# The last pair of heads of an attention layer: four half phases made into two whole ones

## The chip, the cores and the metric

One core of a Trainium2 chip runs the whole program. The metric is the device time of one execution in microseconds (us). In the text PE is the matmul engine (TensorE), DVE is VectorE, ACT is ScalarE, POOL is GpSimd, and SP is the queue that issues most DMAs. An engine works through its own instruction stream in program order and waits on semaphores for the others.

## What is computed

Two layers on x of shape (2, 1024, 128), each an attention-like part and a feed-forward part, all in fp32. The change lies in the first part of the first layer, full attention with 16 heads of 64 channels over each of the two sequences:

```python
Q = jnp.einsum('btd,hkd->bthk', x, W_Q) + b_Q      # K and V alike, x layer-normed
scores = jnp.einsum('bqhk,bshk->bhqs', Q, K) / jnp.sqrt(d_head)
attn = jax.nn.softmax(scores, axis=-1)
out_h = jnp.einsum('bhqs,bshk->bqhk', attn, V)
x = x + jnp.einsum('bqhk,hdk->bqd', out_h, W_O) + b_O
```

Behind it follow a routed feed-forward part with 8 experts (each row of x goes to one), a state-space part and a dense feed-forward part with 8 experts.

## The kernel before

**Pairs and phases.** Heads are taken two at a time: 8 pairs for each sequence, pairs 0 to 15. Pair 15 is `LAST`. The 1024 queries of a pair are two chunks `c` of 512, and the 1024 keys are eight blocks `j` of 128. A step `("score", pair, c, j)` makes the scores of a key block against a query chunk for both heads of the pair (`pe_score`, eight matmuls, lines 583 and 587). ACT exponentiates them in one instruction of 128x1024 (`act_score`, line 1072) into one of ten buffers `prob`. A step `("pv", pair, c, j)` multiplies them by the values and adds to the output bank `A.O` (`pe_pv`, line 615). After the eighth, `take` copies that bank to `oraw` on ACT (line 1081). One pair and chunk with its eight scores and eight value products is a phase (`phase`).

**Normalising.** The sum over the keys of the exponentials is made elementwise first: seven additions of 128x1024 for a phase, one for each `j` from 1 to 7. POOL makes them for pairs 0 to 14 (`pool_score`, line 2014) and DVE for pair 15 (`dve_late_sums`, line 1690, run at the place of the step `pv` in DVE's order). `("sumhalf", pair, c)` is a set of 32 very small matmuls over that sum (`pe_sum_half`, line 665), which needs all seven additions, and a reciprocal on DVE (line 1542). `("out", pair, c)` is the output projection (`pe_out`, line 679, 16 small matmuls) and eight DVE instructions that scale it by the reciprocal and add it to x (`dve_out`, line 1556).

**Order.** One list, `K.order`, written out by hand, says in which order every engine takes its steps: each engine walks the same list and runs what is its own. So moving a step in the list moves it in the stream of PE, of DVE, of ACT, of POOL and of SP. For pairs 0 to 14 a phase has eight scores and then eight value products, with other steps between the value products. These include the projections and maxima for later pairs. The last pair has none of those left. Its list is written by `last_phase(f)` for f = 0 to 3: four scores, four value products, each time. The two output projections of pair 14 both stand behind the scores of f = 1.

**Side steps of the routed part.** Between the value products stand steps from `EARLY` for the routed feed-forward of the first sequence: `turn` is a transpose of gathered rows on PE (line 732), `turned` its copy by ACT (line 1156), and `fetch` is a DMA of an expert's weights, 578 KB, issued by SP (line 2194). Fetches 6 to 12 also wait for a score of pair 15 each (`FETCH_BEHIND`).

**Banks.** PSUM is used as four double banks, slots 0 to 3. Scores and output projections of pair 15 turn through slots 0, 1 and 2 (`slot_of`), and each waits until ACT or DVE has emptied what was in its slot before. The single bank 7 serves `turn`, `sumhalf` and the like one after another.

**After the last pair.** `routed_order` goes on with this list:

```python
order = [("after", "scores"), ("up", 0), ("gelu", 0), ("sumhalf", LAST, 1), ("lnhalf", 3), ("out", LAST, 1), ("up", 1), ("gelu", 1),
         ("fetch", 13), ("after", "attention"), ("pad",), ("lnvar", 3), ("lnroot", 3), ("down", 0), ("yrow", 0), ("fetch", 14)]
```

`up` and `down` are an expert's two products (lines 745 and 756), `yrow` adds a bias on DVE (line 1662). `lnhalf` and `lnvar` are DVE's statistics of x for the layer norm of the second sequence (lines 1464, 1452 and 1456). `lnroot` on POOL and `lnrows` on DVE (line 1473) finish it, and `lnturn` on PE (line 569) transposes the normed rows.

Of the kernel before, what the change touches and what calls it, by code (L numbers as in the profile page):

```python
# [16 lines left out]
NT = SEQ // P  # L17
AT = B * NT
CH = 512
NC = SEQ // CH  # L20
# [48 lines left out]
LAST = PAIRS - 1  # L69
# [109 lines left out]
def turned(n):  # L179

    return [("lnturn", n, 0), ("lnturn", n, 1), ("lncopy", n, 0), ("lncopy", n, 1)]
# [6 lines left out]
def largest(*maxes):  # L188

    return [step for m in maxes for step in (("max", *m), ("maxed", *m))]  # L190


def phase(pair, c):


    last, nxt, ahead = pair - 1, pair + 1, pair + 2
    maxes = [(nxt, *m) for m in MAXES[NT * c:NT * (c + 1)]]
    chunks = [chunk for chunk in CHUNKS[2 * c:2 * c + 2] if ahead < PAIRS and (ahead, *chunk) not in STAGED]
    first, second = ([*map(lambda chunk: project(ahead, chunk), chunks)] + [[], []])[:2]
    pv = [("pv", pair, c, j) for j in range(NT)]  # L200
    early = [EARLY.get((pair, 2 * c + i), []) for i in range(2)]
    order = []
    for j in range(NT):
        order += largest(maxes[j]) + [("score", pair, c, j)]
    if c == NC - 1:
        order.append(("cols", nxt))
    if last >= 0:
        order.append(("out", last, c))
    order += first[:1] + pv[:1] + first[1:] + pv[1:3] + second[:1] + pv[3:4] + second[1:] + pv[4:5]
    if c == NC - 1:  # L210
        order += [("row", nxt), ("rowed", nxt)] + pv[5:6] + [("values", nxt, 1), ("valued", nxt, 1)] + early[0] + pv[6:7] + [("sumhalf", pair, 0)]
    else:
        order += [("values", nxt, 0), ("valued", nxt, 0)] + pv[5:6] + early[0] + pv[6:7] + [("sumhalf", last, NC - 1)] * (last >= 0)
    return order + pv[7:] + [("take", pair, c)] + early[1]


def slot_of(step):

    kind, pair, *k = step
    if kind == "max" and pair:  # L220
        return 0 if k[0] % 2 == 0 else 3
    if kind == "score" and pair < LAST:
        return 1 + k[1] % 2
    if kind == "out" and pair < LAST - 1:
        return 0
    if kind == "score":
        return (2 + k[1]) % 3 if k[0] == 0 else k[1] % 3
    if kind == "out":
        return (2, 0)[k[0]] if pair == LAST else 1 + k[0]


def last_phase(f):

    pair, c, js = LAST, f // 2, range(NT // 2 * (f % 2), NT // 2 * (f % 2 + 1))
    order = [("score", pair, c, j) for j in js]
    if f == 1:
        order += [("out", pair - 1, 0), ("out", pair - 1, 1)]
    second = ([("sumhalf", pair, 0)] if f == 3 else []) + EARLY.get((pair, f), [])
    pv = [("pv", pair, c, j) for j in js]
    order += pv[:2] + second + pv[2:3] + [("sumhalf", pair - 1, NC - 1)] * (f == 0) + pv[3:]  # L240
    if f % 2:
        order.append(("take", pair, c))
    if f == 3:
        order.append(("out", pair, 0))
    return order


def ahead_of_scores(pair, chunk):
    return [("proj", pair, *chunk), ("full", pair, *chunk)]


def attention_order():

    order = [("gsum",), ("lnvar", 0), ("lnroot", 0), ("gscale",), ("lnrows", 0), *turned(0), ("bias", 0)]
    keys, queries, more_keys, more_queries = (("proj", 0, *ch) for ch in CHUNKS)
    maxes = [(0, *m) for m in MAXES]
    order += [keys, queries, *largest(*maxes[:2]), more_keys, more_queries, *largest(*maxes[2:4])]
    order += [("full", 0, *ch) for ch in CHUNKS] + largest(maxes[4]) + ahead_of_scores(1, CHUNKS[0]) + largest(*maxes[5:7])
    order += ahead_of_scores(1, CHUNKS[1]) + largest(*maxes[7:9]) + [("values", 0, 0)] + largest(*maxes[9:11])
    order += ahead_of_scores(1, CHUNKS[2]) + largest(*maxes[11:13]) + ahead_of_scores(1, CHUNKS[3]) + largest(maxes[13])  # L260
    order += [("values", 0, 1)] + largest(maxes[14]) + ahead_of_scores(2, CHUNKS[0]) + largest(maxes[15])
    order += [("gdir",), ("cols", 0), ("row", 0), ("valued", 0, 0), ("rowed", 0), ("valued", 0, 1)]
    for pair in range(LAST):
        for c in range(NC):
            order += phase(pair, c)
    for f in range(4):
        order += last_phase(f)
    return order


# [116 lines left out]
def whole_order():  # L387
    return attention_order() + routed_order() + first_inputs_order() + recurrence_order() + dense_order()
# [48 lines left out]
def plan_all(K):  # L437
# [7 lines left out]
    for step in K.order:  # L445
# [15 lines left out]
        elif step == ("after", "state"):  # L461
            work.take_turns(0, 6)
            for bank in range(2, 8):
                work.held.pop(bank, None)
        elif kind == "score":
            plan_slot(K, "act", step, slot_of(step))
            if k[2]:
                (K.psum_late if k[0] == LAST else K.psum_done).plan(*k)
        elif kind == "max":
            plan_slot(K, "dve", step, slot_of(step) if k[0] else 1 + len(K.slots.place) % 2, now=False)  # L470
        elif kind == "maxed":
            K.slots.plan_empty("max", *k)
        elif kind == "out":
            plan_slot(K, "dve", step, slot_of(step))
        elif kind in ("sumhalf", "gdir"):
            work.plan("dve", *step)
# [2046 lines left out]
```

## Time and profile before

| | before |
|---|---|
| median of three runs | 1172.74 us |
| the three runs | 1172.57, 1172.74, 1174.8 us |
| the profiled execution: its own time | 1174.9 us |
| its span in the profile | 1173.6 us |
| mean granted TensorE clock in it | 0.983 |
| PE busy | 1099.0 us, 94% of the span |
| DVE busy | 828.6 us, 71% |
| ACT busy | 619.2 us, 53% |
| POOL busy | 761.6 us, 65% |

The profile is of one execution, the table's third row, and its times count from the span's start. The last pair of heads takes the stretch from 707.26 to some 749 us. Start and duration of matmuls come from the profile, their ends are modelled, so the distance from one start to the next is the better measure.

### The profile page before, as it was taken

What the parts mean: (1) busy time and instruction counts of PE and PEld (TensorE: products, weight loads), DVE (VectorE), ACT (ScalarE), POOL (GpSimd) and SP (SyncE); (2) the same over time, 40 slices, a digit from 0 to 9 for tenths busy, and PEclk for the clock granted to TensorE, in tenths of its full rate; (3) what the DMA queues carried; (4) which work ended last, traced back from release to release, by engine and by line L of the source; (5) the groups of instructions that cost most, each with busy time, mean ns of one, the idle gap of its engine ahead of it and who ended that gap; (6) DMA issues with size and microseconds to landing.
All of it is one profiled execution on the core that took longest, in us unless ns stands there. A gap on an engine that the chain in (4) does not pass through costs nothing.

```text
span 1173.6 us, 19598 instructions
## 1 busy us (share of the span) xinstructions
PE 1099.0 (94%) x7549; PEld 676.2 (58%) x7549; DVE 828.6 (71%) x1223; ACT 619.2 (53%) x867; POOL 761.6 (65%) x393
## 2 busy tenths in 40 slices
PE   5899998999999998999999999978879988899998
PEld 1456565556556565556665655877535434445786
DVE  4757665667657666656676755624798999998887
ACT  3545354535435445535443534545985664856753
POOL 3588877687877877686778980041289897996200
PEclk9999998999999999999999999989899999999999
DMA  6000000000000000000000115356564444341000
GB/s 202 2 1 2 1 1 1 2 1 1 2 1 1 2 1 1 2 1 2 1 1 7 44 40 198 106 169 206 161 213 144 161 148 141 130 164 47 11 9 18
DMA packets 38076, 68.85 MB, mean 59 GB/s; under 512 B 5952, under 2 KB 24128, under 8 KB 37984
## 3 DMA queue, kind: packets, MB, share of 16 engines
q1 hardware_dynamic: 34976, 64.52, 17.2%
q0 software_dynamic: 1024, 2.10, 0.5%
q8 instruction: 60, 0.98, 0.3%
q10 hardware_dynamic: 1984, 0.98, 0.3%
q14 instruction: 32, 0.26, 0.1%
HBM read 61.30 MB, written 6.16 MB: 57 GB/s over the span
## 4 chain that ended last, share of the span: by engine, by line
PE 73%; POOL 8%; issue 7%; DVE 7%; ACT 3%; DMA 2%; POOLq 0%; SPq 0%; ACTq 0%; DVEq 0%
PE psum L615 18%; PE psum L583 14%; PE psum L599 5%; PE psum L631 5%; PE psum L587 5%; PE psum L981 3%; PE psum L887 3%; POOL psums L2014 3%; PE psum L964 3%; PE psum L665 2%; POOL hc L2102 2%; PE psum L679 2%; PE psum L646 2%; DVE mx L1501 2%; PE psum L756 2%
## 5 line engine op out<-in xcount | busy, mean ns | idle before, releaser
L2014 POOL TENSOR_TENSOR psums<-psums,prob 128x1024 f32<-128x1024 f32 x180 | 427.8, 2377 | 26.7 <-POOL psums L2014 1.3
L1501 DVE TENSOR_REDUCE mx<-psum 128x2 f32<-128x1024 f32 x256 | 300.9, 1225 | 55.6 <-PE psum L599 55.1
L1072 ACT ACTIVATE prob<-psum 128x1024 f32<-128x1024 f32 x256 | 261.5, 1027 | 70.2 <-PE psum L587 47.2
L615 PE MATMUL psum<-prob,V 128*64 128x512 f32 x1024 | 246.4, 597 | 0.0
L2102 POOL TENSOR_TENSOR hc<-hs,cc 128x1024 f32<-128x1024 f32 x64 | 151.7, 2371 | 21.2 <-DVE hs L1789 18.6
L2014 POOL TENSOR_TENSOR psums<-prob 128x1024 f32<-128x1024 f32 x30 | 72.1, 2404 | 122.7 <-ACT prob L1072 122.7
L1789 DVE TENSOR_TENSOR_SCAN hs<-dA,psum 128x1024 f32<-128x1024 f32 x64 | 146.4, 2287 | 2.2
L615 PEld LDWEIGHTS psum<-prob,V 128*64 128x64 f32 x1024 | 67.7, 137 | 102.1 <-issue 98.2
L887 PE MATMUL psum<-hc,ident 128*128 128x512 f32 x256 | 123.3, 605 | 2.5 <-DVE slot_rows_h L1797 1.4
L583 PE MATMUL psum<-q_hi,k_hi 64*128 64x512 f32 x512 | 108.6, 411 | 8.4 <-ACT prob L1072 8.4
L599 PE MATMUL psum<-k_hi,q_hi 64*128 64x512 f32 x512 | 110.0, 418 | 4.5 <-DVE mx L1501 1.6
L587 PE MATMUL psum<-guard,row_one 64*128 64x512 f32 x512 | 104.7, 395 | 0.7 <-DMA guard<-mrow 0.7
L1081 ACT COPY oraw<-psum 128x512 f32<-128x512 f32 x32 | 18.8, 588 | 163.1 <-PE psum L615 163.1
L583 PE MATMUL psum<-q_hi,k_lo 64*128 64x512 f32 x512 | 104.8, 396 | 0.0
L583 PE MATMUL psum<-q_lo,k_hi 64*128 64x512 f32 x512 | 104.8, 396 | 0.0
L1556 DVE SCALAR_TENSOR_TENSOR x<-psum,inv,x 128x128 f32<-128x128 f32 x256 | 72.0, 345 | 21.4 <-PE psum L679 15.5
L599 PEld LDWEIGHTS psum<-k_hi,q_hi 64*128 64x128 f32 x512 | 51.6, 189 | 42.6 <-issue 27.1
L887 PEld LDWEIGHTS psum<-hc,ident 128*128 128x128 f32 x256 | 48.5, 193 | 44.6 <-issue 32.4
L583 PEld LDWEIGHTS psum<-q_hi,k_hi 64*128 64x128 f32 x512 | 49.9, 188 | 41.8 <-ACT prob L1072 26.1
L871 PE MATMUL psum<-xdr,pickr 128*128 128x512 f32 x128 | 57.7, 533 | 10.8 <-DVE hs L1789 10.6
L1494 DVE SCALAR_TENSOR_TENSOR q_lo<-psum,bq,q_hi 128x512 fp32r<-128x512 f32 x28 | 21.0, 751 | 60.8 <-ACT q_hi L1046 60.8
L1046 ACT ACTIVATE q_hi<-psum,bq 128x512 fp32r<-128x512 f32 x32 | 22.0, 689 | 78.6 <-PE psum L631 78.6
(287 smaller groups left out, 1746.6 us busy)
## 6 DMA issues: line engine op xcount, KB each, us to landing
cc<-C_rows SPq DMA_DIRECT2D x64, 512.0 KB, 3.7
kq_wts<-in_e_rows SPq DMA_DIRECT2D x14, 578.0 KB, 4.9
e_wts<-in_e_rows SPq DMA_DIRECT2D x10, 578.0 KB, 4.5
e_w<-in_e_rows SPq DMA_DIRECT2D x6, 578.0 KB, 4.8
slots_in<-e_zero SPq DMA_DIRECT2D x2, 960.0 KB, 8.4
slots_out<-e_y SPq DMA_DIRECT2D x30, 64.0 KB, 3.2
x<-in_x SPq DMA_DIRECT2D x2, 512.0 KB, 4.9
e_w<-in_e_w SPq DMA_DIRECT2D x1, 1024.0 KB, 7.7
```

Of the source, the lines that this page charges most:

```text
L583: pe.matmul(both[:, s, :], left[HALF[s], js], right[HALF[s], cs], start=(part == 0), stop=False)
L587: ins = pe.matmul(both[:, s, :], A.row_one[HALF[s], :], A.guard[q][HALF[s], cs], start=False, stop=True)
L599: ins = pe.matmul(both[:, s, :], A.q_hi[r][HALF[s], t * P:(t + 1) * P], A.k_hi[r][HALF[s], c * CH:(c + 1) * CH], start=True, stop=True)
L615: ins = pe.matmul(A.O[HALF[s], :], A.V[pair % 2][:, j, s * DH:(s + 1) * DH], A.prob[unit(pair, c, j) % NPB][:, s * CH:(s + 1) * CH], start ...
L631: ins = pe.matmul(bank[HALF[s], :], w[:, (2 * p + s) * DH:(2 * p + s + 1) * DH], K.xnT[:, b, c * CH:(c + 1) * CH], start=True, stop=True)
L887: ins = pe.matmul(X.Y[:, c * CH:(c + 1) * CH], K.ident[:, :], X.hc[u % 3][:, c * CH:(c + 1) * CH], start=(u > 0 and n == 0), stop=(n == NS ...
L1072: act.activation(A.prob[n % NPB][:, :], slots.bank("score", pair, c, j).rearrange("p s n -> p (s n)"), ACT.Exp, scale=float(DH) ** -0.5).t ...
L1501: dve.tensor_reduce(K.A.mx[:, :, t, c], slots.bank("max", pair, t, c), AXX, ALU.max).then_inc(*slots.inc("max", pair, t, c))
L1556: ins = dve.scalar_tensor_tensor(out=K.x[:, tile, :], in0=slots.bank("out", pair, c)[:, s, t * P:(t + 1) * P], scalar=A.inv[:, s * NT + 4 ...
L1789: dve.tensor_tensor_scan(X.hs[u % 3][:, :], X.dA[u % 3][:, :], X.gain[u % 2], 0.0, ALU.mult, ALU.add).then_inc(X.state_done, 1)
L2014: pool.tensor_tensor(total[:, :], (K.A.prob[(n - 1) % NPB] if j == 1 else total)[:, :], K.A.prob[n % NPB][:, :], ALU.add).then_inc(*K.psum ...
L2102: pool.tensor_tensor(X.hc[u % 3][:, :], X.hs[u % 3][:, :], X.cc[u % NCC][:, :], ALU.mult).then_inc(X.product_done, 1)
```

## The change

The last pair gets two phases. Each has all eight scores, then one output projection of pair 14, then eight value products. The side steps are the same ones, put between these value products. The reciprocal sums of pair 14 and 15 and the copies stay at the same value products or move by one. The slots change with it: scores of chunk 0 take slot j % 3 where they took (2 + j) % 3, and both output projections of pair 14 take slot 2 where they took 1 and 2.

```diff
     if kind == "score":
-        return (2 + k[1]) % 3 if k[0] == 0 else k[1] % 3
+        return k[1] % 3
     if kind == "out":
-        return (2, 0)[k[0]] if pair == LAST else 1 + k[0]
-
-
-def last_phase(f):
-
-    pair, c, js = LAST, f // 2, range(NT // 2 * (f % 2), NT // 2 * (f % 2 + 1))
-    order = [("score", pair, c, j) for j in js]
-    if f == 1:
-        order += [("out", pair - 1, 0), ("out", pair - 1, 1)]
-    second = ([("sumhalf", pair, 0)] if f == 3 else []) + EARLY.get((pair, f), [])
-    pv = [("pv", pair, c, j) for j in js]
-    order += pv[:2] + second + pv[2:3] + [("sumhalf", pair - 1, NC - 1)] * (f == 0) + pv[3:]
-    if f % 2:
-        order.append(("take", pair, c))
-    if f == 3:
-        order.append(("out", pair, 0))
-    return order
+        return (2, 0)[k[0]] if pair == LAST else 2
+
+
+def last_phase(c):
+
+    pair = LAST
+    order = [("score", pair, c, j) for j in range(NT)]
+    pv = [("pv", pair, c, j) for j in range(NT)]
+    early = [EARLY[pair, 2 * c + i] for i in range(2)]
+    if c == 0:
+        return order + [("out", pair - 1, 0)] + pv[:2] + early[0] + pv[2:3] + [("sumhalf", pair - 1, NC - 1)] + pv[3:5] + early[1] + pv[5:] + [("take", pair, c)]
+    order += [("out", pair - 1, 1)] + pv[:2] + [("sumhalf", pair, 0)] + early[0] + pv[2:6] + early[1] + pv[6:]
+    return order + [("take", pair, c), ("out", pair, 0)]
...
-    for f in range(4):
-        order += last_phase(f)
+    for c in range(NC):
+        order += last_phase(c)
```

## Rows read from the trace of the kernel before

**Rows 1.** The page: its first line.

```profile
span 1173.6 us, 19598 instructions
```

**Rows 2.** Busy time by stretch: us, PE, PEld, DVE, ACT, POOL, clock, DMA share, GB/s.

```profile
707.26:726.30 19.04, 19.04 (x170) 11.35 (x168) 8.26 (x21) 9.22 (x11) 0.00 (x0) 1.00 0.67 228
726.30:742.11 15.81, 15.81 (x131) 8.90 (x129) 12.30 (x12) 8.14 (x9) 0.00 (x0) 1.00 0.37 113
```

**Rows 3.** The chain of waits behind the last pair: start, duration, what.

```profile
746.18 0.39 DVE stats L1464 x2
...
746.58 1.14 DVE x L1556 x4
...
754.84 0.66 PE psum L569 x4
...
781.34 3.84 DMA slots_out<-e_y
```

**Rows 4.** PE in order of time, pair 15: start, duration, line, tiles.

```profile
716.41 0.51 PE L583 MATMUL psum<-q_hi,k_hi 64*128 64x512 f32 x2
...
717.46 0.40 PE L583 MATMUL psum<-q_hi,k_hi 64*128 64x512 f32 x2
...
720.21 1.95 PE L679 MATMUL psum<-wo,oraw 64*128 64x128 f32 x32
722.09 1.94 PE L615 MATMUL psum<-prob,V 128*64 128x512 f32 x8
723.95 0.55 PE L732 MATMUL psum<-ident,slot_rows_h 128*128 128x128 f32 x3
...
726.30 0.50 PE L583 MATMUL psum<-q_hi,k_hi 64*128 64x512 f32 x2
...
730.15 3.65 PE L615 MATMUL psum<-prob,V 128*64 128x512 f32 x16
733.74 0.50 PE L583 MATMUL psum<-q_hi,k_hi 64*128 64x512 f32 x2
...
742.11 1.16 PE L679 MATMUL psum<-wo,oraw 64*128 64x128 f32 x16
...
744.28 1.10 PE L665 MATMUL psum<-ones,psums 128*64 128x1 f32 x32
745.31 1.16 PE L679 MATMUL psum<-wo,oraw 64*128 64x128 f32 x16
```

**Rows 5.** PE in order of time, a single output projection in phase 14.

```profile
695.37 1.07 PE L679 MATMUL psum<-wo,oraw 64*128 64x128 f32 x16
696.36 4.51 PE L615 MATMUL psum<-prob,V 128*64 128x512 f32 x20
```

**Rows 6.** DVE in order of time.

```profile
721.72 4.48 DVE L1556 SCALAR_TENSOR_TENSOR x<-psum,inv,x 128x128 f32<-128x128 f32 x16 [4.80 <-issue]
726.12 5.20 DVE L1690 TENSOR_TENSOR psums<-psums,prob 128x1024 f32<-128x1024 f32 x4
731.24 1.22 DVE L1690 TENSOR_TENSOR psums<-prob 128x1024 f32<-128x1024 f32 x1
...
740.45 0.21 DVE L1542 RECIPROCAL inv<-psum 128x8 f32<-128x8 f32 x1 [1.86 <-PE psum L665]
740.58 2.51 DVE L1690 TENSOR_TENSOR psums<-psums,prob 128x1024 f32<-128x1024 f32 x2
743.37 2.29 DVE L1556 SCALAR_TENSOR_TENSOR x<-psum,inv,x 128x128 f32<-128x128 f32 x8 [0.28 <-PE psum L679]
```

**Rows 7.** ACT in order of time, the exponentials of four scores.

```profile
727.53 3.78 ACT L1072 ACTIVATE prob<-psum 128x1024 f32<-128x1024 f32 x4 [0.53 <-PE psum L587]
```

**Rows 8.** PE in order of time, just ahead of a stretch at half clock.

```profile
574.61 2.08 PE L708 MATMUL psum<-e_wgu,xnT 128*128 128x8 f32 x16
```

**Rows 9.** Busy time by stretch, as rows 2, at full and at half clock.

```profile
576.60:580.00 3.40, 3.40 (x19) 2.68 (x20) 2.86 (x8) 0.84 (x1) 0.00 (x0) 0.54 0.00 0
703.00:706.00 3.00, 2.12 (x34) 1.35 (x32) 0.69 (x1) 0.59 (x1) 2.86 (x2) 1.00 0.26 58
```

## The prediction

> **What bounds the kernel now.** I read the page first, then the busy time of the last pair's stretch, then the chain of waits behind it, and last the streams of PE, DVE and ACT one by one. The span is 1173.6 us [rows 1], and the profiled execution took 1174.9 us by its own time, 1.3 more than its span. That is 2.2 above the median of the three runs, at the top of their range. I work out a difference against this execution and put it on the median.
>
> In pair 15 PE never rests: it is busy in all 19.04 us of the first stretch and in all 15.81 us of the second, at the full clock [rows 2]. So up to the last value product every 0.1 us of PE counts. DVE has 8.26 busy us in the first stretch and 12.30 of 15.81 in the second. The reader is to see that DVE is no bound as a share, but has little left in the second. From 746.18 the chain has left PE: it runs over DVE's statistics, DVE's last output projection (746.58) and the layer norm until PE's transposes at 754.84 [rows 3]. What makes DVE late in that stretch makes the kernel late. The chain goes on through the routing of the second sequence to the store of the last expert row at 781.34, and those steps hang on each other, so I see no slack there.
>
> **What goes from PE.** No matmul is removed. What goes is changing between kinds of matmul. A score costs 0.917 us in a run ((720.21 - 717.46) / 3), but the first costs 1.05 [rows 4]. Four scores and the change to value products take 730.15 - 726.30 = 3.85. Four value products take 3.59 before scores follow. Two in the middle cost 3.59 - 1.86 = 1.73, with 1.86 from 722.09 to 723.95, so 0.865 each. Two half phases are 2 x (3.85 + 3.59) = 14.88. One whole is 3.85 + 4 x 0.917 + 3.59 + 4 x 0.865 = 14.57. That is 0.31 saved for each chunk, 0.62 in all. The two projections of pair 14 took 1.88 together (720.21 to 722.09). A single one takes 0.99 [rows 5], so two cost 1.98, and I count 0.05 of that 0.10 as a change that the scores no longer pay (3.80 into a projection, 3.85 into a value product). PE gains 0.57, call it 0.6. Bounds: 0.3 if only one side of each change is saved, 0.9 if the parts around the transposes gain too.
>
> PE would then start the second phase's scores at 726.30 - 0.31 (one phase merged) - 0.89 (one projection moved behind, 1.88 - 0.99) = 725.1, and its projection of pair 15 at 742.11 - 0.57 = 741.5.
>
> The Trainium skill, "TensorEngine Tiling (Array Packing)", section Key Properties, says that changing the tiling mode drains TensorE. By that rule alone, which speaks for the change, the kernel would be faster by the drains; the trace agrees in sign, and the sum by its own rows is the 0.6 above. This is the rival "gain" below.
>
> **What moves on DVE.** This decides. In the new list the projection of (14, 1) stands behind eight scores and ahead of all value products of chunk 1. DVE runs the seven additions of the chunk at the places of the value products. So all seven are queued behind DVE's part of that projection, though the first exponentials are there 6 us earlier. Before, both projections stood in the first chunk, and DVE started chunk 1's additions at 731.24 [rows 6].
>
> Step by step: eight scores from 725.1 take 3.80 + 4 x 0.917 = 7.47, so PE's projection starts at 732.57. DVE starts 1.26 after such a start (742.11 to 743.37, with an idle 0.28 ended by PE) [rows 4, 6], at 733.8. Eight of its instructions take (726.12 - 721.72) / 2 = 2.20, to 736.0. An addition has a pitch of (731.24 - 726.12) / 4 = 1.28, seven take 8.96, and the reciprocal among them takes 0.13 (740.45 to 740.58). Then DVE comes to the projection of (15, 0) at 745.1. Before it was 743.37. That is 1.7 later. With the first chunk DVE is done in time: its projection starts at about 716.0, seven additions and a reciprocal end at 727.3, and it then idles for 6.5 us.
>
> Who waits: PE comes to the last `sumhalf` at 741.5 + (744.28 - 742.11) = 743.7 and needs the last addition at 745.1, so PE idles 1.4. It starts its last projection some 1.03 later (744.28 to 745.31), at 746.1, and DVE could take that at 747.4. DVE itself is ready only 746.58 - 743.37 = 3.21 after 745.1, at 748.3. So the 1.4 on PE is not added to the 1.7; the chain of rows 3 starts 1.7 late, and with it `lnrows`, the transposes at 754.84 and all that follows. The part of PE's 0.6 that is gained ahead of DVE's last projection start is already in the 1.7, through the 725.1. Sum: +1.7. Bounds: +1.3 (DVE starts 0.1 sooner after PE, PE gains 0.9) and +2.1 (PE gains 0.3, DVE 0.1 slower).
>
> **Edits that cost nothing.** ACT takes 3.78 / 4 = 0.945 for an exponential [rows 7], a little more than a score on PE. Over eight scores it falls 0.2 behind. A score needs only the exponential three before it: the eighth starts 6.5 after the first, and that exponential ends 1.23 + 5 x 0.945 = 5.96 after it (1.23 from 726.30 to 727.53). The margin is 0.5; if it goes, PE waits by what is missing. Slot 2 for the projection needs the sixth exponential, 6.9 after the first score, and PE comes at 7.47. The second transpose and the reciprocal share bank 7: PE needs it at about 721.7 and DVE's reciprocal is done at about 721. If that were late, PE would lose the lateness. The slots of chunk 0 were empty long before. The weight fetches on SP keep their order and only come sooner, since the scores that they wait for do. DMA share is 0.67 and 0.37 in the two stretches [rows 2], and the first use of the earliest of them is in the sixth expert slot behind the pair.
>
> **The rivals.** (1) Likeliest, 0.60: DVE is late, +1.7, so 1174.4 us, 0.14% over the median, inside what is told from no change (0.2%, 2.3 us).
>
> (2) Gain, 0.15: the additions are no bound, because DVE starts them sooner than I reckon or because what follows absorbs 1.7. For it speaks DVE's idle time; against it that DVE's stream is in order and that rows 3 show no idle step up to 781.34. It would show -0.6, 1172.1 us. It decides if DVE's additions end before 743.7.
>
> (3) The other side, 0.20: slower by more than 0.2%, through the clock. PE's idle 1.4 at 743.7 is followed by `sumhalf`, 32 matmuls of one column. In the trace PE did 2.0 us of 128x8 matmuls at 574.61 [rows 8], and then came 3.4 us at a granted clock of 0.54 [rows 9], near the lower of the two levels (1.2 GHz, not 2.4). Against it: an idle 0.9 in the stretch 703 to 706 (PE busy 2.12 of 3.00) left the clock at 1.00. If 3.4 us at half clock fall behind 754.84, where PE is in the chain, they cost half of that, 1.7, and the sum is +3.4: 1176.1 us. If they fall at once behind the wait, DVE's chain hides most (PE has 748.3 - 747.4 = 0.9 to spare there), and the sum stays near +2.1. It decides when the added cost passes 0.6.
>
> The Trainium skill, "TensorE: Matmul & The Clock Gate", section "Part 1: The HAM clock gate", says that the clock is halved after idling and regained by sustained work. The trace agrees at rows 9, and nothing before the change shows what it makes of a wait like this one.
>
> (4) The remaining 0.05: something else, such as the exponentials or bank 7 holding PE by several tenths in each phase, or a transfer that comes in another order downstream.
>
> **How the numbers follow.** The time is that of the first case, 1172.74 + 1.7 = 1174.4. The runs shown lie 2.2 apart, so a median may sit 1 to 2 us off. The range goes from just under the gain to just over the third case: 1171.9 to 1176.8. Slower by over 0.2%: 0.17 from case 3, 0.12 from the upper end of case 1, 0.01 else: 0.30. Faster: 0.03 from case 1 and 0.05 from case 2: 0.08. Within: 0.62.
>
> **What would show it.** Right if in the profile after, PE's second phase starts at about 725.1, DVE idles about 6.5 us ahead of the second projection, its last addition ends near 745.1, the last `sumhalf` on PE has an idle time of about 1.4 ended by line 1690, and the transposes of line 569 that ended the chain start near 756.5. Wrong if the additions start ahead of DVE's projection, if PE idles within the eight scores (line 1072 as the releaser), or if the granted clock falls between 743 and 760. The time would be wrong, with the steps right, if the distance from 754.84 to the end changes by more than 1 us.

## The result and the profile after

The changed kernel takes 1175.17 us (median of 12 runs, 1173.87 to 1177.46); the kernel before, beside it on the same chip, 1172.65 us (12 runs, 1168.91 to 1174.8). The ratio is 1.0026, 95% interval 1.0013 to 1.0038. It is 0.26% slower, some 3 us (the two medians lie 2.5 apart), a little past the 0.2% that I had set as the bound of no change. The interval reaches from 0.13 to 0.38%, so on which side of that bound it lies is not settled. The forecast was 1174.4 with 62% on no change and 30% on slower.

The page after, its first line:

```profile
span 1173.7 us, 19598 instructions
```

That is within 0.1 us of the span of before [rows 1], and would mislead. In this execution the pair's first score starts at 704.83, before it started at 707.26, although the same work stands ahead of it. So I measure from that first score. I call S its start and T the start of the second transpose of the layer norm, where the chain leaves DVE for PE. Before, T - S is 754.84 - 707.26 = 47.58 us. After, it is 754.37 - 704.83 = 49.54. From S to the end it was 466.34 and is 468.87, 2.53 more: 1.96 up to T, 0.57 behind it.

Line numbers of the kernel after are four smaller than those of before in this part, so its 1686 is 1690 before. PE after, in order of time (start, duration, line, tiles, and in brackets the idle time and what ended it):

```profile
704.83 0.50 PE L579 MATMUL psum<-q_hi,k_hi 64*128 64x512 f32 x2
...
705.87 0.41 PE L579 MATMUL psum<-q_hi,k_hi 64*128 64x512 f32 x2
...
711.33 0.41 PE L579 MATMUL psum<-q_hi,k_hi 64*128 64x512 f32 x2
...
712.24 1.07 PE L675 MATMUL psum<-wo,oraw 64*128 64x128 f32 x16
...
722.56 0.49 PE L579 MATMUL psum<-q_hi,k_hi 64*128 64x512 f32 x2
...
729.96 1.05 PE L675 MATMUL psum<-wo,oraw 64*128 64x128 f32 x16
730.94 1.94 PE L611 MATMUL psum<-prob,V 128*64 128x512 f32 x8
732.71 1.05 PE L661 MATMUL psum<-ones,psums 128*64 128x1 f32 x32
733.61 5.35 PE L611 MATMUL psum<-prob,V 128*64 128x512 f32 x24
738.89 1.16 PE L675 MATMUL psum<-wo,oraw 64*128 64x128 f32 x16
739.98 1.16 PE L741 MATMUL psum<-slotT,e_wts 128*128 128x128 f32 x8
742.57 1.10 PE L661 MATMUL psum<-ones,psums 128*64 128x1 f32 x32 [1.43 <-DVE psums L1686]
743.60 1.16 PE L675 MATMUL psum<-wo,oraw 64*128 64x128 f32 x16
744.69 2.08 PE L741 MATMUL psum<-slotT,e_wts 128*128 128x128 f32 x8
746.56 1.80 PE L752 MATMUL psum<-e_wts,slot_rows_h 128*128 128x128 f32 x8
748.20 1.06 PE L741 MATMUL psum<-slotT,e_wts 128*128 128x128 f32 x8
```

Eight scores and a projection go through without an idle step. The projection of (15, 0) starts 738.89 - 704.83 = 34.06 after S, where it was 34.85 [rows 4]. Then PE idles 1.43 for the last addition, and two steps behind that its matmuls take double. The `up` at 744.69 lasts 1.87 to the next start, and the one at 748.20 lasts 0.89.

DVE after:

```profile
713.42 2.29 DVE L1552 SCALAR_TENSOR_TENSOR x<-psum,inv,x 128x128 f32<-128x128 f32 x8 [9.18 <-PE psum L675]
...
718.27 6.54 DVE L1686 TENSOR_TENSOR psums<-psums,prob 128x1024 f32<-128x1024 f32 x5
731.12 2.29 DVE L1552 SCALAR_TENSOR_TENSOR x<-psum,inv,x 128x128 f32<-128x128 f32 x8 [6.31 <-PE psum L675]
733.32 1.22 DVE L1686 TENSOR_TENSOR psums<-prob 128x1024 f32<-128x1024 f32 x1
...
734.64 7.87 DVE L1686 TENSOR_TENSOR psums<-psums,prob 128x1024 f32<-128x1024 f32 x6
742.43 2.28 DVE L1552 SCALAR_TENSOR_TENSOR x<-psum,inv,x 128x128 f32<-128x128 f32 x8
```

The reader is to see the 6.31 of idle time ended by PE's projection, with all seven additions behind it. DVE comes to the projection of (15, 0) at 37.60 after S, where it was 36.11 [rows 6].

The busy time by stretch, first up to the last value product's end and then to T (us, PE, PEld, DVE, ACT, POOL, clock, DMA share, GB/s), and a narrower stretch behind the wait:

```profile
722.56:738.89 16.33, 16.33 (x146) 10.10 (x144) 9.57 (x16) 8.03 (x9) 0.00 (x0) 1.00 0.38 110
738.89:754.37 15.48, 13.84 (x143) 13.16 (x141) 13.02 (x48) 7.75 (x23) 2.05 (x4) 0.89 0.31 89
...
744.80:748.20 3.40, 3.40 (x17) 3.40 (x17) 3.26 (x15) 1.14 (x4) 0.14 (x2) 0.51 0.48 135
```

Granted clock 0.51: that is the lower level, 1.2 GHz. The chain of waits shows what it did:

```profile
743.67 1.09 PE psum L675 x16
744.76 2.00 PE psum L741 x8
746.77 1.59 PE psum L752 x8
...
751.04 0.91 PE psum L752 x8
...
751.97 0.29 DVE e_y L1658
752.26 2.06 DVE xrows L1469 x8
```

Before, the chain in this place ran over DVE and POOL alone, from 746.18 to 754.80. Rows 3 leave out these two pieces of it:

```profile
750.94 1.68 POOL rstd L1964
752.64 2.15 DVE xrows L1473 x8
```

Now it runs over PE at half clock: DVE's bias step for an expert row (line 1658) stands ahead of `lnrows` in DVE's stream and waited for PE's `down`.

### The profile page after: what moved, and what is told of

Read it like the earlier page. It is cut to its first block, busy times and chain, and to the rows that moved or that the text cites. A ratio compares the mean times of both kernels' runs of the same rounds, so it can differ in the third digit from the quotient of the medians.

```text
span 1173.7 us, 19598 instructions
## 1 busy us (share of the span) xinstructions
PE 1098.3 (94%) x7549; PEld 677.3 (58%) x7549; DVE 827.8 (71%) x1223; ACT 618.0 (53%) x867; POOL 760.8 (65%) x393
## 4 chain that ended last, share of the span: by engine, by line
PE 72%; POOL 8%; DVE 8%; issue 7%; ACT 3%; DMA 2%; POOLq 0%; SPq 0%; DVEq 0%; ACTq 0%
PE psum L611 17%; PE psum L579 14%; PE psum L595 5%; PE psum L627 5%; PE psum L583 5%; PE psum L977 3%; PE psum L883 3%; POOL psums L2010 3%; PE psum L960 3%; POOL hc L2098 3%; PE psum L661 2%; PE psum L642 2%; PE psum L675 2%; DVE mx L1497 2%; PE psum L752 2%
```

## The experiments

The experiments ran on three chips: e1 to e4 on one, where the kernel before took 1178.68 us (median of 35 runs), e5 to e8 on a second (1179.81, 35 runs), and e9 to e12, one run each, on a third, where the one run of the kernel before took 1180.76. In the groups of 35 the kernel before ran from 1175.3 to 1181.5. Ratios are against it on the same chip. Since that scatter is as large as the effects, T - S in each profile is the finer measure. Up to T it repeats to within 0.05 us wherever the clock stays full. The kernel before has a profile on the first chip only. e4 has its order on PE, and there PE comes to the projection of (15, 0) 34.80 us after S, where before has 34.85.

| run | ratio, 95% interval | PE's wait | clock behind it | T - S |
|---|---|---|---|---|
| before | | none | full | 47.58 |
| changed, first | 1.0026 [1.0013, 1.0038] | 1.43 | half, 3.4 us | 49.54 |
| e1 changed again | 1.0016 [1.0001, 1.0031] | 1.43 | full | 48.94 |
| e8 changed, third | 0.9999 [0.9985, 1.0014] | 1.42 | half, 6.8 us | 51.07 |
| e9 changed, fourth | one run | 1.42 | half, 3.4 us | 49.49 |
| e2 DVE's additions first | 0.9983 [0.9969, 0.9996] | none | full | 46.79 |
| e7 the same again | 0.9987 [0.9971, 1.0002] | none | full | 46.74 |
| e3 up fills the wait | 1.0003 [0.9990, 1.0016] | 0.53 | full | 48.94 |
| e10, e11 the same | one run each | 0.54, 0.53 | full | 48.95, 48.90 |
| e4 before, DVE late by two additions | 1.0015 [1.0000, 1.0031] | none at sumhalf | full | 49.69 |
| e5 half phases, projection moved | 1.0006 [0.9995, 1.0017] | none | full | 48.12 |
| e6 whole phases, projection in chunk 0 | 0.9993 [0.9982, 1.0004] | none | full | 47.05 |
| e12 changed, longer wait | one run | 2.69 | half, 6.8 us | 52.07 |

**e1, e8, e9: the changed kernel again.** No edit.

> The changed kernel again, for a second profile beside the others. Theory 1 (DVE's additions stand behind its projection, and PE's wait for them lowers the clock): from the start of the pair's first score DVE comes to the projection of (15, 0) at 37.6 us, PE waits 1.4 us ahead of the last sumhalf, and a stretch of half clock begins within 3 us of that wait, as in the first profile. Total 2 to 3 us over the kernel before. Theory 2 (the stretch of half clock there was chance): the same 37.6 and 1.4, the clock stays full behind the wait, and the total is still 2 to 3 us over.

> The changed kernel a third time. The transposes at 48.9 to 49.0 us after the first score if the clock stays full behind PE's wait, and at 49.5 if it falls there, which happened once in two profiles. Total 1.4 to 3 us over before.

> The changed kernel, a fourth profile, for the clock behind PE's wait alone. In three profiles the wait was 1.43 us each time, and in two of them a stretch of half clock began within 3 us behind it, of 3.4 and 6.8 us. Theory 1 (the wait brings it, by where it falls): again a wait of 1.43, and a stretch of half clock in about two of three. Rival (chance, anywhere): none.

DVE's lateness and PE's wait came the same each time: 37.60, 37.59, 37.59, 37.59 us after S, and 1.42 or 1.43. The clock did not. In e1 it stayed full, as theory 2 of the first expectation had it; in e8 and e9 it fell, as in theory 1. In e1 T - S was 48.94, which is 1.36 over before. In e8 it fell for 6.8 us, from 0.8 us behind the end of the wait:

```profile
743.98 1.24 PE L661 MATMUL psum<-ones,psums 128*64 128x1 f32 x32 [1.42 <-DVE psums L1686]
745.15 2.08 PE L675 MATMUL psum<-wo,oraw 64*128 64x128 f32 x16
747.15 2.07 PE L741 MATMUL psum<-slotT,e_wts 128*128 128x128 f32 x8
749.02 1.91 PE L752 MATMUL psum<-e_wts,slot_rows_h 128*128 128x128 f32 x8
...
757.32 0.66 PE L565 MATMUL psum<-ident,xrows 128*128 128x128 f32 x4 [0.21 <-DVE xrows L1469]
```

T - S of e8, 51.07, lies outside both values that I had expected for it. So what the change costs up to T is 1.36 for DVE and 0, 0.6 or 2.1 for the clock. The timing of e8 (0.9999, its upper end 1.0014) came out lower than I expected, and its median of 1180.04 lower than its own profiled run (1182.45). Its interval still meets those of the other two timings, that of the first only by a hair, and the three together (mean of all runs less the mean of the kernel before: 3.0, 1.6 and 0.4 us) agree with 1.4 to 3 only loosely.

**e2, e7: DVE alone in another order.** PE, ACT and SP are those of the changed kernel. DVE alone takes two steps behind the last addition: its part of the projection of (14, 1) and the reciprocal of (15, 0). No run moves one without the other.

```diff
+def dve_order(order):
+
+    late = [("out", LAST - 1, 1), ("sumhalf", LAST, 0)]
+    order = [step for step in order if step not in late]
+    at = order.index(("pv", LAST, NC - 1, NT - 1)) + 1
+    return order[:at] + late + order[at:]
...
-    for kind, *k in K.order:
+    for kind, *k in dve_order(K.order):
```

> PE, ACT and SP keep the new order. DVE alone takes the seven additions of the last chunk before its part of the projection of (14, 1) and the reciprocal of (15, 0). Theory 1: DVE's additions end about 30.5 us after the pair's first score, PE waits nowhere and keeps full clock, the projection of (15, 0) is bound by PE at 34.1 + 1.2 = 35.3, and the kernel is 0.6 to 0.8 us faster than before, some 3 faster than the changed one. Rival (the loss comes from the runs of eight scores or from the clock by chance, not from DVE's order): the time stays within 1 us of the changed kernel, 2 to 3 over before.

> The kernel of the second experiment again: its first timing gave 0.17% under before, 2.0 us, and its trace only 0.8 us at the layer norm's transposes. Theory 1: the transpose again at 46.8, and the time 0.5 to 1 us under before, so that two timings together lie nearer 0.8 than 2. Rival (a gain elsewhere too): again 2 us.

DVE in e2:

```profile
727.76 1.23 DVE L1686 TENSOR_TENSOR psums<-prob 128x1024 f32<-128x1024 f32 x1 [0.96 <-ACT prob L1068]
729.09 7.87 DVE L1686 TENSOR_TENSOR psums<-psums,prob 128x1024 f32<-128x1024 f32 x6
736.88 2.28 DVE L1552 SCALAR_TENSOR_TENSOR x<-psum,inv,x 128x128 f32<-128x128 f32 x8
...
742.15 2.29 DVE L1552 SCALAR_TENSOR_TENSOR x<-psum,inv,x 128x128 f32<-128x128 f32 x8 [2.87 <-issue]
```

The additions now wait for an exponential and not for the projection. They end 30.1 after S in place of 37.7. DVE then idles 2.87 ahead of the projection of (15, 0). The profile names no releaser there, but the start lies 1.27 behind PE's, as it does where PE is named (1.26 in rows 4 and 6). PE has no idle step up to the transposes, and T - S is 46.79: 0.79 less than before and 2.15 less than in e1. The two timings give 0.9983 and 0.9987, 2.0 and 1.5 us under before; only the first excludes 1, and its interval includes 0.8 us. So my expectation for e7 missed: the two together lie nearer 2 than 0.8. Whether something behind T gains too is open. Up to T the order of DVE's steps alone turns a gain of 0.79 into a loss of 1.36. The rival that the runs of eight scores cost something falls.

**e3, e10, e11: PE's wait filled, DVE as late as ever.**

```diff
-    order = [("after", "scores"), ("up", 0), ("gelu", 0), ("sumhalf", LAST, 1), ("lnhalf", 3), ("out", LAST, 1), ("up", 1), ("gelu", 1),
+    order = [("after", "scores"), ("up", 0), ("gelu", 0), ("up", 1), ("gelu", 1), ("sumhalf", LAST, 1), ("lnhalf", 3), ("out", LAST, 1),
```

> The changed kernel with the second expert's up and gelu ahead of the last sumhalf, so that PE has 1.1 us of matmuls in the 1.4 us of its wait. DVE's lateness is untouched. Theory 1: PE's idle time falls to about 0.3, the clock stays full, the transposes of the layer norm come 0.5 us sooner (49.0 in place of 49.5 us after the pair's first score), the kernel is 0.5 to 1 us faster than the changed one and still 1.5 slower than before. Rival (DVE's lateness costs nothing, the PE wait is the whole loss): at most 0.5 slower than before.

> The kernel with the second up ahead of the last sumhalf, second profile. DVE's lateness is the same, PE's wait 0.5. Theory 1: full clock from the last pair to the transposes at 48.9. Rival: half clock as often as in the changed kernel.

> The same kernel, third profile: by theory 1 full clock and 48.9 once more.

PE in e3:

```profile
740.95 2.05 PE L741 MATMUL psum<-slotT,e_wts 128*128 128x128 f32 x16
743.53 1.10 PE L661 MATMUL psum<-ones,psums 128*64 128x1 f32 x32 [0.53 <-DVE psums L1686]
...
750.75 1.13 PE L752 MATMUL psum<-e_wts,slot_rows_h 128*128 128x128 f32 x8 [1.11 <-DVE e_y L1658]
```

T - S is 48.94, the same as in e1, though 0.9 of the wait is gone. The time that PE won came back as a wait for DVE at the third `down`, 1.11 where e1 has 0.36 there. So up to T PE's wait costs nothing in itself; DVE's lateness is what is paid. The timing does not decide this: it is 0.03% over before, 0.4 us, where I expected 1.5 and the rival at most 0.5, and its interval (-1.2 to +1.9 us) holds both. The idle time fell to 0.53 and not to the 0.3 that I expected, and my expectation of a T at 49.0 compared with the profile at half clock. The clock stayed full in all three.

**e4: DVE late and nothing else.** The kernel before, with two idle additions behind the last:

```diff
+    if (c, j) == (NC - 1, NT - 1):
+        dve.wait_ge(*K.psum_late.at(pair, c, j))
+        for _ in range(2):
+            dve.tensor_tensor(A.psums[0][:, :], total[:, :], A.prob[n % NPB][:, :], ALU.add).then_inc(*K.dve_own.inc())
+            dve.wait_ge(*K.dve_own.now())
```

> The kernel before, with two more additions of 128x1024 on DVE behind the last one, ahead of its projection of (15, 0); their result is read by nobody. PE's sumhalf does not wait for them. Theory 1 (the chain behind the pair runs over DVE): 2 x 1.3 - 0.3 of slack = 2.3 us slower. Rival (what follows absorbs DVE's lateness; only PE's wait costs): within 0.5 of before.

```profile
744.14 2.48 DVE L1695 TENSOR_TENSOR psums<-psums,prob 128x1024 f32<-128x1024 f32 x2
746.66 2.29 DVE L1556 SCALAR_TENSOR_TENSOR x<-psum,inv,x 128x128 f32<-128x128 f32 x8
```

DVE's projection starts 38.34 after S, 2.23 later than before, and T comes 2.11 later. So DVE's lateness in this place is paid nearly in full at T (2.11 of 2.23), in the old order too. The time agrees (0.15%, 1.8 us), but its interval reaches down to 0 and so does not shut out the rival; T - S does. PE's last `sumhalf` had no wait here, which separates DVE's part from PE's.

**e5: the projection moved, the half phases kept.**

```diff
-    if f == 1:
-        order += [("out", pair - 1, 0), ("out", pair - 1, 1)]
+    if f in (1, 2):
+        order.append(("out", pair - 1, f - 1))
```

> The kernel before with its four half phases, but the projection of (14, 1) stands behind the first scores of chunk 1, ahead of all value products of that chunk, as in the changed kernel. Theory 1 (it is the run of eight scores ahead of the projection, with the additions queued behind it, that makes DVE late): DVE's projection of (14, 1) starts some 23 us after the pair's first score and the last addition still ends at about 35.9, so the second transpose of the layer norm stays at 47.6 us, within 0.2, and the time within 0.2% of before. Rival (the place of the projection alone is enough): the transpose at 49 and 1.4 us slower.

```profile
730.91 2.29 DVE L1556 SCALAR_TENSOR_TENSOR x<-psum,inv,x 128x128 f32<-128x128 f32 x8 [1.77 <-PE psum L679]
...
743.97 2.29 DVE L1556 SCALAR_TENSOR_TENSOR x<-psum,inv,x 128x128 f32<-128x128 f32 x8 [0.28 <-PE psum L679]
```

DVE waits 1.77 for the moved projection, not 6.31, and at the last one it is DVE that waits for PE again, by 0.28. So the place of the projection alone does not make DVE the bound. My expectation for T missed: 48.12, 0.54 later than before and not within 0.2. PE itself was late: the projection stood in a slot whose exponential was not done, and waited 0.32. The other 0.22 of the 0.54 no run assigns.

```profile
729.66 1.16 PE L679 MATMUL psum<-wo,oraw 64*128 64x128 f32 x16 [0.32 <-ACT prob L1072]
```

**e6: the list alone, for all engines.** Whole phases, with the projection of (14, 1) in chunk 0 and the `sumhalf` of (15, 0) behind the sixth value product of chunk 1. That is its place in the kernel before; the change had put it behind the second, a move by four, where the section on the change speaks of one at most.

```diff
-        return order + [("out", pair - 1, 0)] + pv[:2] + early[0] + pv[2:3] + [("sumhalf", pair - 1, NC - 1)] + pv[3:5] + early[1] + pv[5:] + [("take", pair, c)]
+        return order + [("out", pair - 1, 0)] + pv[:2] + early[0] + pv[2:3] + [("sumhalf", pair - 1, NC - 1), ("out", pair - 1, 1)] + pv[3:5] + early[1] + pv[5:] + [("take", pair, c)]
-    order += [("out", pair - 1, 1)] + pv[:2] + [("sumhalf", pair, 0)] + early[0] + pv[2:6] + early[1] + pv[6:]
+    order += pv[:2] + early[0] + pv[2:6] + [("sumhalf", pair, 0)] + early[1] + pv[6:]
```

> The changed kernel with its two whole phases, but the projection of (14, 1) stands in chunk 0 behind the sumhalf of (14, 1), and the sumhalf of (15, 0) behind the sixth value product of chunk 1, for all engines. Theory 1: DVE's additions of chunk 1 follow the exponentials and end at 35.4 us at the latest, PE does not wait, the second transpose comes at 46.8 to 47.1, 0.5 to 0.8 sooner than before, total 0 to 1 us faster than before. Rival (the gain in the DVE-only reorder was something else): the transpose at 48.9 as in the changed kernel.

```profile
739.63 0.21 DVE L1538 RECIPROCAL inv<-psum 128x8 f32<-128x8 f32 x1 [3.48 <-PE psum L661]
739.75 2.51 DVE L1686 TENSOR_TENSOR psums<-psums,prob 128x1024 f32<-128x1024 f32 x2
742.55 2.29 DVE L1552 SCALAR_TENSOR_TENSOR x<-psum,inv,x 128x128 f32<-128x128 f32 x8 [0.29 <-PE psum L675]
```

The additions end 35.29 after S and T - S is 47.05, both as expected. It lies 0.26 behind e2; PE comes to its projection of (15, 0) 34.31 after S, 0.25 later than there. That two more changes between kinds of matmul cost this, at the projection among the value products, is argued and not shown. The time, 0.9993 [0.9982, 1.0004], is not told from before.

**e12: the wait made longer.** The changed kernel with one such idle addition ahead of the last real one:

```diff
+    if (c, j) == (NC - 1, NT - 1):
+        dve.tensor_tensor(A.psums[0][:, :], total[:, :], A.prob[n % NPB][:, :], ALU.add).then_inc(*K.dve_own.inc())
+        dve.wait_ge(*K.dve_own.now())
```

> The changed kernel with one more addition of 128x1024 on DVE ahead of the last one of the last chunk; its result is read by nobody. PE's wait should be 1.43 + 1.3 = 2.7 us. Theory 1: DVE's projection of (15, 0) at 38.9, the transposes at 50.2 with the full clock, and half clock behind the wait more surely than with 1.43, which puts the transposes at 51 or later. Rival (the wait has nothing to do with the clock): 50.2.

```profile
744.83 1.87 PE L661 MATMUL psum<-ones,psums 128*64 128x1 f32 x32 [2.69 <-DVE psums L1689]
746.63 2.08 PE L675 MATMUL psum<-wo,oraw 64*128 64x128 f32 x16
```

The clock is already half in the `sumhalf` itself (it fell at 744.4, 0.4 us before the wait ended), and T - S is 52.07, 1.9 over the 50.2 that DVE's lateness alone would give.

## Why the prediction was nearly right, and where it fell short

**DVE's queue: right, and the main cause.** The step said that DVE comes to its projection of (15, 0) 1.7 late with PE idle for 1.4. It measured 37.60 - 36.11 = 1.49 late, with PE idle for 1.43, and at full clock 1.36 of it was paid at T (e1). DVE's idle time ahead of the second projection was 6.31, forecast 6.5. e2 takes away the queueing alone, and the loss is gone; e4 gives DVE's lateness alone, and the loss is there.

**PE's gain: right in kind, too small in size.** The term was 0.57 and measured 34.85 - 34.06 = 0.79. Of the 0.22 that I missed 0.11 came in each chunk. The second phase started 722.56 - 704.83 = 17.73 after S, where the step gives 725.1 - 707.26 = 17.84, and its projection 16.33 after that, where the step gives 16.44. A score inside the long run took (711.33 - 705.87) / 6 = 0.910, not 0.917. So PE came to the projection of (14, 1) 25.13 after S, 0.18 sooner than the step's 732.57 - 707.26. DVE started 1.16 behind PE there (729.96 to 731.12), not 1.26. The two make DVE late by 1.49 and not by 1.7. That the gain is real shows in e2 and e7, where T - S is 0.79 and 0.84 under before.

**The clock: the step that failed.** A fall of the clock between 743 and 760 was one of my own signs of being wrong. I gave slower by the clock 0.20, with a price of 1.7 behind 754.84 and of 0.4 at once behind the wait. It fell in three of four profiles of the changed kernel, 0.8 to 2.1 us behind the end of the wait, and in e12. It fell in none of the three with the wait filled, nor in this place in those of before, e2, e4, e5, e6 and e7: four of the five profiles with a wait of 1.42 and longer, none of the nine without such a wait. I had written that in this place DVE's chain hides most and that the sum stays near 2.1. For a stretch of 3.4 us that was right: 1.96 and 1.91 over before. For 6.8 us it was not: 3.49. The slack of 0.9 that I counted on is used up by the first. The mean of the four profiles at T is 49.76, or 2.2 over before, and not the 1.4 that DVE's queue alone gives. With the 1.7 forecast inside the bound of 0.2% (2.3 us), and a true cost of about 2.2 at T, the two sides of the bound were nearly even. I had them at two to one. And that 1.7 came so near the 1.96 of the first profile is in part luck: DVE alone costs 1.36 there, and the clock, which the 1.7 leaves out, the other 0.6.

The Trainium skill, "TensorE: Matmul & The Clock Gate", section "Part 1: The HAM clock gate", says that idling halves the clock. The runs agree in kind only: the idle 1.43 ahead of a small `sumhalf` was followed by it in three of four, the idle 2.69 in the one profile that there is. That the same 1.43 left it full in e1 means that the length of the wait does not decide alone. An idle 1.11 ahead of a `down` left it full in e3, e10, e11 and e4. What else decides is open: no run moved the wait in time with its length kept.

**What stays open.** The 0.57 between T and the end in the first pair of profiles, and the size of the total: three timings gave 0.26, 0.16 and -0.01%. Behind T other stretches of half clock fall in every execution, and not in the same places, so the profile does not say whether any of them belongs to the change. From T to the end the twelve profiles of the experiments took 421.4 to 424.3 us, and those of one and the same kernel lie up to 2.1 apart; 0.57 is not told from that.

## What to carry to other kernels

When steps are moved in one list that all engines walk, read each engine's queue on its own. Here PE's order became better by 0.8 us, and the same move put seven additions of DVE, the first of which could start 7.5 us sooner (20.94 after S in e2, 28.49 here), behind a step that waited 6.3 us for PE. An engine that idles long and is late afterwards is the sign of it, and reordering that engine alone is both the test and the cure. A wait of PE that costs nothing by the chain can still cost through the clock, so fill it with matmuls where there are any. Here that rests on three profiles with the wait filled against four without, and the timings do not tell the two apart.

## What the runs showed of the hardware beyond that

The start of the kernel scatters. The pair's first score came between 704.4 and 708.3 us in 14 profiles of kernels that do the same work up to there. A comparison of two single spans of this kernel can be off by 4 us from that alone, while distances from S to T repeat to 0.05 us at full clock.

A wait of PE of 1.43 us, the same in place and length to 0.01 us, was followed by the half clock in three profiles and not in the fourth, and then for 3.4 or 6.8 us. An `up` of 0.89 us took 1.87 in it (744.69 to 746.56 above).
